# Block attention issued two head pairs at a time, with values copied by VectorE and two banks for the turned probabilities

## What is computed

```python
x = L0_attn_inputs                                    # (2, 1024, 1024), fp32
h = conv_k3(layernorm(x), conv_w) + conv_b            # 3 taps, 1024 -> 768 channels; split in q, k, v of 256
qh, kh, vh = (einsum('btd,dhe->bthe', t, w) + b ...)  # 16 heads of 64, in blocks of 128 tokens (16 blocks)
scores = einsum('bqhe,bkhe->bhqk', qh / 8, kh)        # causal inside a block, softmax over k
o = einsum('bhqk,bkhe->bqhe', softmax(scores), vh)
x = x + (einsum('bqhe,hed->bqd', o, wo) + bo) @ proj_w + proj_b
x = x + ffn(layernorm(x))      # y = x W_base^T + b_base, plus 4 experts of rank 8 weighted by a softmax gate
```

## Time and profile before

| | us |
|---|---|
| median of 3 runs | 822.52 (820.74 to 822.99) |
| the profiled execution, its own time | 821.56 |
| its span, first to last instruction | 819.7 |
| TensorE busy | 790.8 (96%) |
| VectorE busy | 463.6 (57%) |
| ScalarE busy | 407.5 (50%) |
| POOL busy | 196.7 (24%) |
| convolution's split units | 117.28 to 256.61 |
| attention: first Q to the last projection's start | 256.61 to 606.25 |

### The profile page before, as it was taken

The page is one execution under the profiler, slowest core; times in us unless marked ns, Lnnn a source line. Parts: engine busy times, 40 slices in busy tenths (PEclk is TensorE's granted clock), DMA queues, the critical chain, the costliest instruction groups (busy, mean ns, idle before and its releaser), DMA issues.

```text
span 819.7 us, 14315 instructions
## 1 busy us (share of the span) xinstructions
PE 790.8 (96%) x5248; PEld 704.1 (86%) x5248; DVE 463.6 (57%) x1359; ACT 407.5 (50%) x1085; POOL 196.7 (24%) x184
## 2 busy tenths in 40 slices
PE   3899999999999999999999999999999999999997
PEld 3798887777778788888888888888789999999996
DVE  6899966778877643333333434444684444444441
ACT  5953342344335997676868686867750111111010
POOL 2300103223230434252525253432300010100000
PEclk9999999999999999999999999999999999999999
DMA  8745833533436221211252411202143231313201
GB/s 333 254 123 173 261 121 114 205 120 110 155 141 239 88 106 39 105 39 72 94 235 84 114 62 49 90 1 104 67 139 108 75 104 52 103 52 103 73 31 52
DMA packets 41369, 94.03 MB, mean 115 GB/s; under 512 B 9299, under 2 KB 18387, under 8 KB 40020
## 3 DMA queue, kind: packets, MB, share of 16 engines
q1 hardware_dynamic: 38996, 84.73, 31.0%
q0 software_dynamic: 2304, 8.39, 2.5%
HBM read 66.63 MB, written 26.08 MB: 113 GB/s over the span
## 4 chain that ended last, share of the span: by engine, by line
PE 78%; DVE 11%; ACT 5%; issue 3%; POOL 2%; DMA 0%; DVEq 0%; ACTq 0%; POOLq 0%
PE net_psum L63 15%; PE net_psum L65 15%; PE net_psum L64 15%; PE net_psum L1208 10%; PE net_psum L1275 5%; PE net_psum L1294 4%; PE net_psum L1286 4%; POOL raw L478 2%; PE net_psum L1192 2%; PE net_psum L1326 2%; PE net_psum L1327 2%; PE net_psum L1340 2%; PE net_psum L1328 2%; DVE raw L891 1%; DVE raw L892 1%
## 5 line engine op out<-in xcount | busy, mean ns | idle before, releaser
L63 PE MATMUL net_psum<-fw_hi,xT_hi 128*128 128x354 f32 (+1 forms) x384 | 126.0, 328 | 0.4 <-DVE fw_lo L1059 0.4
L65 PE MATMUL net_psum<-fw_hi,xT_lo 128*128 128x354 f32 (+1 forms) x384 | 124.4, 324 | 0.0
L64 PE MATMUL net_psum<-fw_lo,xT_hi 128*128 128x354 f32 (+1 forms) x384 | 124.2, 324 | 0.0
L495 POOL TENSOR_TENSOR pr<-pr,rrec 128x512 f32<-128x512 f32 x64 | 66.7, 1042 | 219.9 <-DVE rrec L958 213.5
L631 ACT ACTIVATE pr<-pr,negmax 128x128 f32<-128x128 f32 x256 | 99.2, 392 | 12.3 <-DVE negmax L965 12.3
L1208 PE MATMUL net_psum<-ua,wa 128*128 128x256 f32 x384 | 85.5, 385 | 2.3 <-DVE ua L849 2.3
L1208 PEld LDWEIGHTS net_psum<-ua,wa 128*128 128x128 f32 x384 | 73.7, 193 | 12.7 <-issue 2.6
L965 DVE CUSTOM_DVE_ANT_0 pr<-net_psum,mask 128x128 f32<-128x128 f32 x256 | 58.8, 287 | 42.6 <-PE net_psum L1275 42.5
L63 PE MATMUL net_psum<-x_hi,w_hi 128*128 128x512 f32 x192 | 77.1, 401 | 3.2 <-DVE w_lo L898 3.0
L63 PE MATMUL net_psum<-c_hi,wqk_hi 128*128 128x256 f32 x256 | 76.8, 300 | 0.4 <-ACT kf L640 0.4
L478 POOL TENSOR_TENSOR raw<-raw 128x512 f32<-128x512 f32 x24 | 37.3, 1557 | 164.5 <-ACT raw L578 164.5
(11 more groups left out here) (174 smaller groups left out, 1824.0 us busy)
## 6 DMA issues: line engine op xcount, KB each, us to landing
wa<-in_conv_w SPq DMA_DIRECT2D x24, 512.0 KB, 4.1
raw<-in_conv_w SPq DMA_DIRECT2D x24, 384.0 KB, 3.4
xn<-in_x SPq DMA_DIRECT2D x16, 512.0 KB, 10.1
xr<-in_x SPq DMA_DIRECT2D x8, 1024.0 KB, 5.0
x_scratch<-xr SPq DMA_DIRECT2D x8, 1024.0 KB, 4.0
x1t<-x_scratch SPq DMA_DIRECT2D x16, 512.0 KB, 4.0
out<-y POOLq DMA_DIRECT2D x16, 512.0 KB, 5.0
c_raw<-c_scratch SPq DMA_DIRECT2D x7, 768.0 KB, 4.7
```

The source lines that it names most:

```text
L63: pe.matmul(out, w_hi, x_hi, start=first, stop=False)
L64: pe.matmul(out, w_hi, x_lo, start=False, stop=False)
L65: return pe.matmul(out, w_lo, x_hi, start=False, stop=last)
L495: pool.tensor_tensor(pr[:, jj % 4], pr[:, jj % 4], rrec[:, jj % 4].unsqueeze(2).to_broadcast([P, UN, P]), ALU.mult).then_inc(s["p_ready"], 1)
```

## The change

Attention runs in 32 double steps (`ND`). Double step D issues on TensorE: S of pairs 2D-2 and 2D-1; P of 2D-6 and 2D-5; T of 2D-4 and 2D-3; Q of 2D; a unit; Q of 2D+1; a unit; A of 2D-6 and 2D-5. So kinds that before stood once in each step stand twice in a row. Of the four double steps of a group, q = 1 and 2 have two V units each and q = 3 and 0 two Y units each. The odd pair is turned into bank 7 (also a unit's bank), `op` has a half bank for each pair, `vf` is copied by VectorE. Waits for scores, for p x v and for `oT_hi` are for both pairs. In double step 2, Q and a unit stand ahead of S and T.

In the first stage VectorE scales tiles 5, 6, 7 (before: 2, 6, 7) and evacuates tile 6 and half of 7, and TensorE issues 18 transposes of the identity (`FILL`) between the last turned tile and the first unit. Ahead of the split units, `low_weight(0)` moves behind `inputs(7)` on VectorE, and `high_weight(1)` and `pre_scale(2)` move ahead of `high_input(7)` on ScalarE. The dense layer's work is placed anew between the last double steps.

```diff
-    DVE_SCALES = (2, LT - 2, LT - 1)
+    DVE_SCALES = (LT - 3, LT - 2, LT - 1)
+    FILL = 18
+    SC, TR, PV = 1, 2, 3
+    def unit(D, k):
+        g, q = D // DG, D % DG
+        e, n = ((g - 2, 2), (g, 0), (g, 2), (g - 1, 0))[q]
+        return (q in (1, 2), e, n + k) if 0 <= e < NG else None
+        ptp = (psum[:, 3], psum[:, 7])
+        op = psum[:, 4].rearrange("p (j b t) -> p j b t", j=2, b=GB)
...
         (ScalarE)
+            def attention_pair(D):
+                g, q = D // DG, D % DG
+                if q == 3 and 0 <= g - 1 < NG:
+                    a_high(g - 1)
+                for jj in pair_of(D - PV):
+                    heads_out(jj)
+                for jj in pair_of(D - TR):
+                    turned_out(jj)
+                for h in range(2):
+                    if D < ND and h == 0:
+                        queries_keys(2 * D)
+                    if pair_of(D - SC):
+                        exponentials(2 * (D - SC) + h)
+                    if 0 < g and g + 1 < NG and q == 1:
+                        c_high(g + 1, h)
+                    if D < ND and h == 1:
+                        queries_keys(2 * D + 1)
...
         (VectorE)
+                for jj in pair_of(D - SC):
+                    masked(jj)
+                    if jj % 2 == 0 and q == 3 and 0 <= g - 1 < NG:
+                        a_low(g - 1)
+                for jj in pair_of(D - PV):
+                    heads_low(jj)
+                unit_out(D, 0)
+                for jj in pair_of(D - SC):
+                    reciprocals(jj)
+                unit_out(D, 1)
...
         (VectorE, ahead of the split units)
-                if c == DC - 2:
-                    low_weight(0)
+            low_weight(0)
+            low_input(DC - 1)
...
         (TensorE)
+            def turns(jj):
+                pe.wait_ge(s["p_ready"], jj + 1)
+                wait(pe, s["pT_ready"], jj - 1)
+                if jj % 2:
+                    emptied(pe, jj // 2 + TR, 1)
+                for un in range(UN):
+                    mm = pe.transpose(ptp[jj % 2][:, un * P:(un + 1) * P], pr[:, jj % 4, un], ident[:])
...
+            def attention_pair(D):
+                if D == 2:
+                    queries_keys(2 * D)
+                    run_unit(D, 0)
+                for jj in pair_of(D - SC):
+                    scores(jj)
+                for jj in pair_of(D - PV):
+                    head_outputs(jj)
+                for jj in pair_of(D - TR):
+                    turns(jj)
+                if D < ND and D != 2:
+                    queries_keys(2 * D)
+                if D != 2:
+                    run_unit(D, 0)
+                if D < ND:
+                    queries_keys(2 * D + 1)
+                run_unit(D, 1)
+                for jj in pair_of(D - PV):
+                    output_sums(jj)
...
+            pe.wait_ge(s["xT_ready"], LT // 2 + 1)
+            for i in range(FILL):
+                pe.transpose(turned(0, LT // 2)[:, 0, i % 4 * P:(i % 4 + 1) * P], ident[:], ident[:])
...
+            for D in range(ND + 1):
+                attention_pair(D)
+            tile_transposes(0)
+            attention_pair(ND + 1)
+            for jj in pair_of(ND - 1):
+                head_outputs(jj)
+            dense(0, 0)
+            for jj in pair_of(ND - 1):
+                output_sums(jj)
+            dense(0, 1)
+            for D in (ND + 3, ND + 4):
+                for k in range(2):
+                    run_unit(D, k)
```

More of the change, by code:

```diff
@@ L307, in qk_acc, with emptied @@
             return qk_side if J in (1, 3) else qkp
-        def is_step(jj):
-            return 0 <= jj < NJ
+        def emptied(eng, D, k):
+            for d in range(D - 1, -1, -1):
+                if unit(d, k):
+                    is_v, e, n = unit(d, k)
+                    eng.wait_ge(s["v_ready" if is_v else "x1_ready"], 4 * e + n + 1)
+                    return
         @block.sync
@@ new lines, in c_high, with a_high @@
+            def c_high(g, h):
+                m = slice(3 * h, 3 * h + 3)
+                act.wait_ge(s["c_loaded"], 16 * g)
+                act.activation(c_hi[g % 2][:, m], c_raw[:, m], ACT.Copy).then_inc(s["c_hi_ready"], 1)
+            def a_high(e):
+                act.wait_ge(s["a_step"], NP * (e + 1))
+                wait(act, s["yy_done"], YT * e)
+                for d in range(WC):
+                    a = act.activation(by_plane(a_hi[:, d]), planes_of(ap_[:, d]), ACT.Identity, bias=bo_c[:, d:d + 1])
+                a.then_inc(s["a_hi_ready"], 1)
@@ new lines, in run_unit, with scores @@
+            def run_unit(D, k):
+                if unit(D, k):
+                    is_v, e, n = unit(D, k)
+                    emptied(pe, D, k)
+                    if k:
+                        wait(pe, s["pT_ready"], min(2 * (D - TR + 1), NJ))
+                    values(e, n) if is_v else projection(e, n)
+            def scores(jj):
+                pe.wait_ge(s["qk_ready"], jj + 1)
+                wait(pe, s["max_ready"], jj // 2 * 2)
+                for b in range(GB):
+                    t = slice(b * P, (b + 1) * P)
+                    o = slice(jj % 2 * GT + b * P, jj % 2 * GT + (b + 1) * P)
+                    for h in range(2):
+                        e = slice(h * DH, (h + 1) * DH)
+                        mm = pe.matmul(scp[:, h, o], qf[e, jj % 2, t], kf[e, jj % 2, t], start=True, stop=True)
+                mm.then_inc(s["sc_done"], 1)
@@ new lines, in output_sums @@
+            def output_sums(jj):
+                j = jj % NP
+                if jj in (0, NP // 2):
+                    pe.wait_ge(s["wo_lo_ready"], 1 if jj == 0 else 2)
+                elif j == 0:
+                    pe.wait_ge(s["a_lo_ready"], jj // NP)
+                pe.wait_ge(s["oT_lo_ready"], jj + 1)
+                for d in range(WC):
+                    o = ap_[:, d]
+                    col = slice(d * P, (d + 1) * P)
+                    pe.matmul(o, wo_hi[:, j, col], oT_hi[:, jj % 2], start=j == 0 and d == 0, stop=False, skip_group_check=True)
+                    pe.matmul(o, wo_hi[:, j, col], oT_lo[:, jj % 2], start=False, stop=False, skip_group_check=True)
+                    mm = pe.matmul(o, wo_lo[:, j, col], oT_hi[:, jj % 2], start=False, stop=j == NP - 1, skip_group_check=True)
+                mm.then_inc(s["a_step"], 1)
```

524 lines of the change are left out of this document (219 added, 305 removed).

## The result

The changed kernel takes 811.36 us (median of 4 runs, 810.68 to 812.35), the kernel before 822.00 in the same session: a ratio of 0.9875, 95% interval 0.9861 to 0.9889. The forecast was 807, range 802 to 813. The profiled execution took 811.95 us with a span of 810.2, against 821.56 and 819.7: 9.5 us less of span where 15.0 were forecast.

What follows compares the result with a forecast made beforehand. TensorE's own sequence was taken to bound the kernel. Savings of 13.4, 1.7 and 3.8 us less losses of 3.2 and 0.7 made 15.0, from 821.56 to 806.6 (807.5 on the median's side); forecast 807 us, range 802 to 813.

Steps and rivals of the forecast that it cites:

- attention, start: Attention up to double step 5: TensorE waits 7.4 us against some 2.0, merged groups return 2.2; 3.2 us lost.
- attention, steady part: 27 double steps from step 10 to 63: 13.8 from entries plus 1.1 idle minus 1.5 waits, 13.4 us saved.
- attention, end: Step 64 to the last projection's start: new waits offset by three merged groups and one unit less; zero change.
- last four Y: After attention, the last four Y wait behind `a_low`, the split of b and the bias sum on VectorE: 0.7 us lost.
- The price of an entry: TensorE's cost at a change of array shape, paid once for two head pairs: 0.51 us saved per double step.
- The waits of S for `kf` beside the high halves: Six double steps with two `c_hi` pieces on ScalarE: S waits 0.25 us each, 1.5 in all.
- has room: Steady part: VectorE, busy 117 of 288 us, can take the `vf` copy at 0.69 us; its waits hold back nobody.
- S(9): Attention start, TensorE's S of pair 9: a wait of 0.4 us, counted in the start's sum.
- First stage: 18 transposes fill TensorE's gap before the first unit and avoid 3.4 us at half clock: 1.7 us saved.
- Ahead of the split units: `inputs(7)` fills VectorE's idle gap, the weight chain comes earlier, TensorE waits less for `w_lo`: 3.8 us saved.
- the fill does not hold the clock: Rival for the first stage: the half clock stays despite the transposes; 808.7 us, chance 0.16.
- The slower rival: Second Q of each double step waits for the first's `qf`/`kf`, past a slack of 0.35 us; 833 us, chance 0.05.

Runs made afterwards that it cites:

- experiment 1: Changed kernel with S, P, T of the even pair, then of the odd pair, in double steps 5 to 31: 824.28 us.
- experiment 6: Changed kernel with the second group's input low halves (`c_lo`) made by VectorE instead of GpSimd, in double step 3: 809.82 us.
- Experiments 3: Changed kernel with the first two feed-forward weight splits two double steps earlier, where GpSimd has no bias sum: 810.12 us.
- Experiment 4: Changed kernel with ScalarE evacuating query and key of the third pair ahead of the turned pairs in double step 2: 810.80 us.
- 8: Changed kernel with several repairs together: Experiments 3, Experiment 4, Experiment 7, A between the Qs of double steps 3 and 4, VectorE side jobs moved: 812.03 us.
- 9: Changed kernel with the repairs of 8, but VectorE's side jobs between reciprocals and behind head outputs, where it waits for exponentials: 802.53 us.
- Experiment 7: Changed kernel with head outputs 60 and 61 made ahead of the feed-forward work on ScalarE and VectorE: 808.86 us.
- experiment 2: Changed kernel without the 18 fill transposes ahead of the first unit (`FILL` = 0): 812.03 us.
- experiment 5: Changed kernel with its conv part undone: first weight's low half ahead of the last inputs, ScalarE's preparations back in the loop: 813.71 us.
- Experiment 11: Changed kernel with the values copied out of their banks by ScalarE, as before, instead of VectorE: 816.31 us.

## Why the prediction was right, and where it was off

The time lies in the range and the direction was right, 4.4 us above the point. That it came so near is in part luck: the start-up gave 1.1 us and the last four Y 0.7 more than forecast, against 7.2 us that the other terms lacked. Term by term, against the profiled executions:

| step of the prediction | forecast | measured |
|---|---|---|
| first stage and ahead of the split units (to the first Q) | 1.7 + 3.8 saved | 4.4 saved |
| attention, start | 3.2 lost | 4.0 lost |
| attention, steady part | 13.4 saved | 10.8 saved |
| attention, end | 0 | 1.7 lost |
| last four Y | 0.7 lost | 0 |
| sum | 15.0 | 9.5 |

- **Steady part.** The step that mattered most holds. The price of an entry follows the shape and is paid once for two pairs: 0.49 us a double step by experiment 1, where the prediction took the upper bound of 0.51. Its terms make a regular double step of 10.10 ((287.69 - 1.1) / 27 - 0.51), and 10.14 were measured: about 1 us of the 2.6 missing. The waits of S for `kf` beside the high halves came nearly as forecast (0.2 each, 0.25 forecast). The other 1.9 are two stalls: S at the head of double step 5, 1.77 instead of 1.09, and 1.2 in double step 31. The second is VectorE's: the sentence that failed there is that with 117 busy of 288 us VectorE "has room". Room on average said nothing of the place where GpSimd runs a long operation with VectorE's beside it. The first is ScalarE's: `kf` of Q(9) stands behind eight exponentials, and S takes 1.77 in experiment 6 as well, where the sums of 1.9 are gone. The prediction had 0.4 of it, in the start's sum as S(9).
- **The memory port.** Experiments 3 and 6 show the cause of those long operations: 3.04 to 1.22 us and 1.9 to 0.28 when GpSimd's operation is not beside them, with the same data and shapes. The Trainium skill, SBUF — State Buffer, Who interferes with whom, says that a VectorE instruction with two SBUF inputs contends with a GpSimd instruction that reads SBUF, and that the port pair that the two share is an exclusive lock. The trace agrees in both places: the VectorE operation ends behind the GpSimd one, 0.15 us for a sum of 0.28 and 1.1 for a split of 1.22. Had I laid the two engines' rows side by side, the 3.68 us of `c_lo` would have stood in the start's sum as VectorE's too.
- **Start of attention.** The waits named were the real ones (the second Q for the first's copy, T ahead of Q(5), Q(8) for `c_lo`). 0.8 us was missing. The wait that the sum did not have is that of A for `oT_lo` in double step 4, 0.94: `oT_lo` stands behind the masks, and the sums that precede the masks took 4.1 us too long (0.9, 1.6 and 1.6). The rest of the 4.1 hid behind the wait for `c_lo`. Experiment 6 takes 0.7 of this wait away. Experiment 4 shows why such sums are fragile, and 8 and 9 what the bound was: not TensorE's 33 us of work, but the place of VectorE's side jobs in its queue.
- **End.** "In the new order TensorE waits some 2.0 for `oT_lo`" is the 2.3 measured. What the forecast set against it, three merged groups and one unit less, did come: without the half clock the stretch takes 25.75 (experiment 4), where 25.4 were forecast. The clock's 1.4 us behind that idle stretch did not stand in the sum. Experiment 7 removes wait and half clock and gains 2.5.
- **First stage.** Up to the first Q 4.4 us came where 5.5 were forecast: 2.77 here instead of 1.7, and 1.65 instead of 3.8 ahead of the split units. The half clock did go, but the one profiled execution without the fill (experiment 2) does not have it either. What kept the clock is open. The rival "the fill does not hold the clock" was wrong on the clock, and that the fill is worth anything is not shown. Besides, the new order lets the first unit start at 24.78 instead of 25.83, 1.05 us that I had put at zero. Together the two, the forecast's 1.7 for the clock and 1.05, make up the start-up's 2.77.
- **Ahead of the split units.** 3.8 forecast, 1.65 measured (experiment 5). The two early waits went, but the stage now begins with one for the first `w_lo`: the chain moved to another place. And four waits at chunk boundaries stay (0.5 to 0.8 from start to start, where 0.23 is a matmul's share, at 154.7, 177.5, 200.2 and 223.3 us). With the 0.11 that the next start loses each time they cost 2.1, of which I had let only 1.0 stand.
- **Last four Y.** Y takes 5.55 in both. The bias sums on VectorE come early enough.
- **The slower rival** (the second Q late in every double step) had, by the estimate, a slack of 0.35 us between it and a loss. In the double step shown above the first Q's `kf` has left the bank at 411.11 and the second Q starts at 411.45, so 0.34 are left, and the estimate of the chain held. Experiment 11 does not test this wait: the `kf` that is late there is the second Q's, which S wants.

## What to carry to other kernels

- Grouping small matmuls of one shape is worth the number of entries that go, here 0.15 to 0.2 us each; count them in the start-to-start times, and then find the buffer that allows it. Without the second bank the same order costs 32 us more.
- Whether a side job fits is a question of its place in the queue, not of the engine's share: behind the last thing that somebody waits for, where the engine waits itself. The same jobs in two places differed by 9.5 us, 2.5 of them by the clock that fell behind the longest wait.
- For every long GpSimd operation look at what VectorE runs at that moment; two-input operations on SBUF data beside it take its time and theirs.

## What the runs showed of the hardware that was not expected

- VectorE operations of 0.28 and 1.2 us with both inputs in SBUF took 1.9 and 3.0 beside GpSimd operations of 1.84 and 2.36 us. Masks, with one input in PSUM and one in SBUF, did not: 70 of the changed kernel's 256 masks ran wholly inside a GpSimd operation of over 0.9 us, at a mean of 0.286 us, and the others took 0.285.
- TensorE's clock stayed at 2.4 GHz after an idle stretch of 2.46 us (experiment 2) and fell to 1.2 GHz after one of 2.35 in the kernel before. At the end it fell in the changed kernel after one of 2.29 (profiled execution) and stayed after one of 2.28 in experiment 4, with the same work ahead of the gap (TensorE busy for 3.87 of 4 us in both). So neither the length of one gap nor how busy TensorE was just before says whether the clock falls; what does is left open. The kernel before differs in the same way, from 819.8 us at a mean clock of 0.999 to 823.0 at 0.995 in one batch, so a difference of 1 to 2 us between two kernels has to be read beside the clock of each execution.
